# VectorE's gated convolution rows and FFN rows ahead of and between the two scans of their step (Mamba layer, one core)

## The chip, the core and the metric

The kernel is one launch on one core of a Trainium2 chip. A core has TensorE (PE in the rows; PEld is its loading of weights), VectorE (DVE), ScalarE (ACT), GpSimd (POOL) and SyncE (SP, which issues transfers here). Each engine works through a list of its own in order; they meet only through semaphores. The metric is the device time of one execution in microseconds (us).

## What is computed

Two layers run over x of 8 sequences x 512 positions x 128 channels, all float32. The first (attention with a gated score, and a mixture of experts) is not touched. The second is a Mamba block times the silu of a quantized FFN:

```python
xv = silu(causal_conv4(xn @ W_in) + conv_b)            # 256 inner channels
ssm = xv @ W_x                                          # 8 dt columns, 16 B, 16 C
delta = softplus(ssm[..., :8] @ W_dt + b_dt)
dA = exp(delta[..., None] * A)                          # A = -exp(A_log), 16 states
dBx = delta[..., None] * B[:, :, None, :] * xv[..., None]
h[t] = dA[t] * h[t-1] + dBx[t]                          # the scan, along the sequence
s = (einsum('bldn,bln->bld', h, C) + xv * D) @ W_out
g = silu((silu(xn @ wg) * (xn @ wu)) @ wd)
x = x + s * g
```

## The kernel before

The Mamba layer handles one sequence b a **round**: round -1 only prepares, rounds 0 to 7 scan, round 8 only ends the last. `rounds` (L1096) writes rounds -1 and 0 out, then a hardware loop whose body is two rounds (executed twice: rounds 1 to 4), then rounds 5, 6, 7 and 8. A round that scans b also **prepares** b+1 (`prep`, rounds 0 to 6: projection by W_x, softplus, delta, du) and **ends** b-1 (`end`, from round 1 on: the last two states and the output).

A round has NP = 8 **steps** q, with two states each (n = 2q and 2q+1) and two halves h of the inner channels. In step q:

- GpSimd multiplies B (replicated over the partitions) with du into `dbx`, two instructions (L1226, out `nfT_all`), one for each half. Between them it has to do, for the round before, three sums of `accP` (L1155) and the output in three instructions (L1163, L1167, L1171), and for the next round `softplus_high` at q = 5 (L1180, waits for ScalarE's `lg`), `softplus_low` at q = 6 (L1184, waits for ScalarE's `e1`, printed `e`), `deltas` at q = 7 (L1192) and `drives`, which makes du, last (L1200).
- ScalarE makes the decays `dA` in PSUM (`decays`, L1394), a step ahead: those of step q+1, two for each half. There are two buffers, so the decays of a half wait for the scan of that half in step q. Behind them in its list stand `scale_state` (L1431, states 5, 7, 9 and 15), `ffn_tanh` (L1444) and parts of the softplus (L1478, L1484, L1488).
- VectorE scans: two instructions (L1644, `TENSOR_TENSOR_SCAN`, out `xnT_all`, a ring of R = 4), one for each half. **Scan 0** and **scan 1** of a step below are these two.
- TensorE projects the states of step q by W_out (`project`, out psum, in `xnT_all`) once both halves are scanned, in step q+1 of its list, 16 matmuls a state (32 in the records, which show each float32 matmul of this size as two). VectorE adds each projected state, times its C column, to `acc` (`add_state`, L1660, four instructions). `project(n)` reuses the bank of state n-2 and waits until that is drained.

Two more kinds of VectorE work are what the change moves:

- **The gated convolution rows**: `conv_gate(h)` (L1670) makes `xv` of sequence b+1 from the tanh and the biased value that ScalarE left (`conv_silu`, L1418 and L1421, semaphore `yh`), one instruction for each half. `conv_silu(., 1)` waits for TensorE's `x_in(., 1)` (psum from `W_taps`), the last thing but the projections of states 14 and 15 in TensorE's round. From `xv` TensorE makes first `ssm()` (W_x), then `skip()` (W_outD), and only then, in step 1, projects states 0 and 1.
- **The FFN rows**: `ffn_hidden(k)`, k = 0, 1, 2 in steps q = 3, 4, 5 (L1710 and L1714), makes block k of the hidden layer from TensorE's `ffn_up(k)` (psum from `wgu`) and ScalarE's tanh `tf` of it. `ffn_up(k+1)` waits for `hf` k+1, that is for L1714; so does `ffn_down` (psum from `wd`) for all three.

The order in each engine's list is written out by hand in the loops over q; the loop of VectorE is the last part of its `round_`.

Of the kernel before, what the change touches and what calls it, by code (L numbers as in the profile page):

```python
# [5 lines left out]
def attention_moe_mamba_ffn(nc, t, out):  # L6
# [25 lines left out]
    KH = DI // P  # L32
# [10 lines left out]
    with ctx:  # L43
# [985 lines left out]
        with ExitStack() as ph:  # L1029
# [547 lines left out]
            def _(dve):  # L1577
# [51 lines left out]
                def round_(b, p, scan, prep, ahead, end):  # L1629
                    def w(n, c):  # L1630
                        dve.wait_ge(S[n], at(b + 1, n, c))

                    def ws(n, c):
                        dve.wait_ge(S[n], at(b, n, c))

                    def scans(q):
                        if not scan:
                            return
                        for h in range(KH):
                            i = 2 * q + h  # L1640
                            ws("dA", i + 1)
                            ws("dbx", i + 1)
                            ws("G", 2 * (q + 1 - 2))
                            nc.vector.tensor_tensor_scan(hring[:, i % R, :, :].rearrange("p n l -> p (n l)"),  # L1644
                                                         dA[:, i % RA, :, :].rearrange("p n l -> p (n l)"),
                                                         dbx[:, i % R, :, :].rearrange("p n l -> p (n l)"),
                                                         0.0, ALU.mult, ALU.add).then_inc(S["scan"], 1)

                    def add_state(b, p, m):

                        dve.wait_ge(S["G"], at(b, "G", m + 1))
                        if m == 0:
                            dve.wait_ge(S["acc0"], at(b, "acc0", 1))
                            dve.wait_ge(S["C"], at(b, "C", 1))
                            dve.wait_ge(S["os"], at(b - 2, "os", 1))
                        i = ON_DVE.index(m)
                        for j in range(TPB):
                            if i:
                                dve.wait_ge(S["acc"], at(b, "acc", (i - 1) * TPB + j + 1))
                            nc.vector.scalar_tensor_tensor(acc[:, p, j, :], bank[Gb[m % 2]][:, j * P:(j + 1) * P],  # L1660
                                                           Cc[:, p, j, m:m + 1],
                                                           acc[:, p, j, :] if i else skip_sb[:, p, j, :],
                                                           ALU.mult, ALU.add).then_inc(S["acc"], 1)

                    def conv_gate(h):
                        if h == 0:
                            w("acc_ps", 0)
                            w("du", 0)
                        w("yh", h + 1)
                        nc.vector.scalar_tensor_tensor(xv[:, h, :], tc_[:, h, :], 1.0, bank[bM[h]],  # L1670
                                                       ALU.add, ALU.mult).then_inc(S["xv"], 1)
# [35 lines left out]
                    def ffn_hidden(k):  # L1707
                        ws("tf", k + 1)
                        ws("hf", k)
                        nc.vector.scalar_tensor_tensor(fa[:, :], tf[:, :], 1.0, bank[bM[0]], ALU.add, ALU.mult)\  # L1710
                            .then_inc(S["fa"], 1)
                        ws("fa", k + 1)
                        ws("dn_ps", 0)
                        nc.vector.scalar_tensor_tensor(hff[:, k, :], fa[:, :], 0.5, bank[bM[1]], ALU.mult, ALU.mult)\  # L1714
                            .then_inc(S["hf"], 1)

                    def gate():
                        ws("tg", 1)
                        dve.wait_ge(S["og"], at(b - 1, "og", 0))
                        nc.vector.scalar_tensor_tensor(G1[:, p, :], tg[:, :], 1.0, bank[bM[1]], ALU.add, ALU.mult)\  # L1720
                            .then_inc(S["G1"], 1)
# [23 lines left out]
                    for q in range(NP):  # L1745
                        if q == 0 and not end:
                            conv_gate(0)
                            conv_gate(1)
                        scans(q)
                        if scan and 3 <= q < 6:  # L1750
                            ffn_hidden(q - 3)
                        if q == 0:
                            if prep and end:
                                conv_gate(0)
                                conv_gate(1)
                            if end:
                                for m in (NS - 2, NS - 1):
                                    if m in ON_DVE:
                                        add_state(b - 1, 1 - p, m)
                        elif scan:  # L1760
                            for m in (2 * q - 2, 2 * q - 1):
                                if m in ON_DVE:
                                    add_state(b, p, m)
                        if scan and q == 6:
                            gate()
# [7 lines left out]
                moments(1)  # L1773
                residual(3)
                rounds(dve, round_)

        run.close()  # L1777
# [41 lines left out]
```

## Time and profile before

| | us |
|---|---|
| median of 3 runs | 787.35 (785.91 to 788.26) |
| the profiled execution, its own time | 789.01 |
| its span, first to last instruction | 787.2 |
| TensorE busy | 667.2 |
| VectorE busy | 664.6 |
| GpSimd busy | 504.5 |
| ScalarE busy | 480.7 |
| layer 2, from round 1 on: VectorE's start of round 1, and the end of the span | 387.08, 787.2 |

The profile is of one execution. Busy time counts only the engine's own operations. A timeline row merges like instructions that follow each other: start, length in us, engine, line, operation, out<-in, count, and in brackets how long the engine sat idle just ahead of it and what released it. Two instructions merged into one row take less than twice the length of one, because the next starts a little before the end of the last: a pair of scans lasts 4.46 and the second starts 2.19 behind the first.

### The profile page before, as it was taken

What the parts mean: (1) busy time and instruction counts of PE and PEld (TensorE: products, weight loads), DVE (VectorE), ACT (ScalarE), POOL (GpSimd) and SP (SyncE); (2) the same over time, 40 slices, a digit from 0 to 9 for tenths busy, and PEclk for the clock granted to TensorE, in tenths of its full rate; (3) what the DMA queues carried; (4) which work ended last, traced back from release to release, by engine and by line L of the source; (5) the groups of instructions that cost most, each with busy time, mean ns of one, the idle gap of its engine ahead of it and who ended that gap; (6) DMA issues with size and microseconds to landing.
All of it is one profiled execution on the core that took longest, in us unless ns stands there. A gap on an engine that the chain in (4) does not pass through costs nothing. (4 is left out here: it accounts for less than half of the span.)

```text
span 787.2 us, 13531 instructions
## 1 busy us (share of the span) xinstructions
PE 667.2 (85%) x3984; PEld 495.5 (63%) x3984; DVE 664.6 (84%) x1182; ACT 480.7 (61%) x942; POOL 504.5 (64%) x292
## 2 busy tenths in 40 slices
PE   1889889999899928797998988888989979987882
PEld 0865556566565513466777777677767768777682
DVE  5968867777566638899999999899999999999992
ACT  1655656666344434978587585685695785874540
POOL 1002661000244552099999999989999999999952
PEclk9999999999999966989999999999999999998896
DMA  8800110003022244622032042042041230420000
GB/s 217 258 1 15 41 40 13 0 0 83 26 74 67 63 69 57 214 109 81 28 130 74 30 148 81 4 148 79 11 164 53 83 116 31 128 76 28 14 1 14
DMA packets 40199, 56.48 MB, mean 72 GB/s; under 512 B 5960, under 2 KB 30032, under 8 KB 40144
## 3 DMA queue, kind: packets, MB, share of 16 engines
q1 hardware_dynamic: 31888, 48.42, 19.1%
q0 software_dynamic: 6528, 6.84, 3.9%
q10 hardware_dynamic: 1728, 0.57, 0.4%
q8 instruction: 24, 0.39, 0.2%
q14 instruction: 31, 0.25, 0.1%
HBM read 46.08 MB, written 9.74 MB: 71 GB/s over the span
## 5 line engine op out<-in xcount | busy, mean ns | idle before, releaser
L1644 DVE TENSOR_TENSOR_SCAN xnT_all<-psum,nfT_all 128x1024 f32<-128x1024 f32 x128 | 285.3, 2270 | 2.7 <-issue 2.4
L1241 PEld LDWEIGHTS psum<-W_out,xnT_all 128*128 128x128 f32 x2048 | 243.8, 196 | 31.0 <-issue 29.0
L1241 PE MATMUL psum<-W_out,xnT_all 128*128 128x128 f32 x2048 | 246.0, 280 | 9.0 <-DVE acc L1660 9.0
L1394 ACT ACTIVATE psum<-delta,A 128x511 f32<-128x511 f32 x256 | 163.3, 678 | 39.2 <-DVE xnT_all L1644 38.4
L1226 POOL TENSOR_TENSOR nfT_all<-nf_rows,du 128x1024 f32<-128x1024 f32 x63 | 146.8, 2358 | 32.7 <-DVE nfT_all L1703 31.5
L1226 POOL TENSOR_TENSOR nfT_all<-attn_all,du 128x1024 f32<-128x1024 f32 x64 | 149.9, 2366 | 0.0
L569 POOL DMA_INDIRECT moe_dram<-xnT_all x40 | 38.3, 957 | 122.2 <-ACT xnT_all L825 122.2
L1660 DVE SCALAR_TENSOR_TENSOR acc<-psum,Cc,acc 128x128 f32<-128x128 f32 x352 | 96.7, 340 | 8.8 <-PE psum L1241 8.8
L558 POOL DMA_INDIRECT xs_dram<-nf_rows,pos x32 | 33.5, 1046 | 75.8 <-DVE pos L879 57.0
L1241 PE MATMUL psum<-vo_all,wgu 128*128 128x512 f32 (+1 forms) x96 | 47.6, 619 | 27.4 <-DVE hff L1714 27.4
L1241 PE MATMUL psum<-vo_all,W_taps 128*128 (+4 forms) x128 | 60.3, 619 | 1.4 <-ACT vo_all L1412 0.7
L618 PEld LDWEIGHTS psum<-vo_all,PT 128*128 128x128 f32 x256 | 31.9, 195 | 25.0 <-ACT PT L777 18.0
L1431 ACT ACTIVATE ts<-psum,Cc 128x128 f32<-128x128 f32 x128 | 35.7, 357 | 13.2 <-PE psum L1241 13.2
L695 PE MATMUL psum<-gud,xnT_all 128*128 x80 | 43.1, 623 | 0.5 <-ACT xnT_all L812 0.5
L1241 PEld LDWEIGHTS psum<-vo_all,wgu 128*128 128x128 f32 x96 | 16.5, 191 | 41.8 <-issue 26.0
L1241 PEld LDWEIGHTS psum<-vo_all,W_taps 128*128 128x128 f32 x128 | 24.3, 199 | 27.8 <-issue 25.8
L618 PE MATMUL psum<-vo_all,PT 128*128 (+1 forms) x256 | 37.7, 291 | 2.6 <-ACT PT L777 2.6
L1418 ACT ACTIVATE tconv<-psum,convb 128x512 f32<-128x512 f32 x16 | 11.0, 687 | 42.7 <-PE psum L1241 42.7
L994 DVE COPY xnT_all<-psum 128x256 f32<-128x256 f32 x40 | 17.0, 424 | 23.4 <-PE psum L707 23.4
L588 PE MATMUL psum<-k_w,q_w 128*128 128x512 f32 x64 | 33.5, 608 | 0.0
L1155 POOL TENSOR_TENSOR accP<-accP,ts 128x512 f32<-128x512 f32 x16 | 20.3, 1271 | 18.0 <-ACT ts L1431 18.0
L1241 PE MATMUL psum<-wd,hff 128*128 128x128 f32 x192 | 23.6, 279 | 8.8 <-DVE hff L1714 8.8
(209 smaller groups left out, 1139.2 us busy)
## 6 DMA issues: line engine op xcount, KB each, us to landing
nf_rows<-bt_dram SPq DMA_DIRECT2D x32, 512.0 KB, 5.2
attn_all<-bt_dram SPq DMA_DIRECT2D x32, 512.0 KB, 3.5
xs_dram<-attn_all SPq DMA_DIRECT2D x4, 645.0 KB, 8.6
xnT_all<-xs_dram SPq DMA_DIRECT2D x40, 64.5 KB
x_all<-in_x_dram SPq DMA_DIRECT2D x8, 256.0 KB, 7.0
res_all<-moe_dram POOLq DMA_DIRECT2D x8, 256.0 KB, 4.5
out_dram<-ow SPq DMA_DIRECT2D x8, 256.0 KB, 2.4
gud<-in_gate_dram SPq DMA_DIRECT2D x1, 1024.0 KB, 5.9
```

The source lines that it names most:

```text
L558: pool.indirect_dma_start(xs_dram, bass.IndirectOffsetOnAxis(ap=pos[:, i:i + 1], axis=0), nf_rows[:, i, :], None).then_inc(s_sc, 16)
L569: pool.indirect_dma_start(moe_dram, bass.IndirectOffsetOnAxis(ap=xs_t[:, u % XN, D:ROW].bitcast(u32), axis=0), yt[:, u % UN, :], None).the ...
L588: nc.tensor.matmul(bank[j % 2], q_w[:, j * P:(j + 1) * P], k_w[:, :], start=True, stop=True)\
L618: ins = nc.tensor.matmul(bank[4][:, j * P:(j + 1) * P], PT[:, j % 2, c, :], vo_all[:, ds(b * TPB + c, 1), :], start=(c == 0), stop=(c == T ...
L695: nc.tensor.matmul(bank[2 + u % 2], xT[:, u % 2, :], gud_flat[:, ds(expert[u], 2 * I)], start=True, stop=True).then_inc(E["gu_ps"], 1)
L1155: nc.gpsimd.tensor_tensor(accP[:, :, :], ts[:, 0, :, :] if i == 1 else accP[:, :, :], ts[:, i, :, :], ALU.add).then_inc(S["accP"], 2 if i ...
L1226: nc.gpsimd.tensor_tensor(dbx[:, i % R, :, :], B_pair(q), du[:, p, h:h + 1, :].to_broadcast([P, 2, L]), ALU.mult)\
L1241: return nc.tensor.matmul(o, l, r, start=start, stop=stop)
L1394: ins = nc.scalar.activation(dA[:, i % RA, k, 1:L], delta[:, p, h, 1:L], ACT.Exp, scale=A[:, h, 2 * q + k:2 * q + k + 1])
L1431: ins = nc.scalar.activation(ts[:, i, j, :], bank[Gb[n % 2]][:, j * P:(j + 1) * P], ACT.Copy, scale=Cc[:, p, j, n:n + 1])
L1644: nc.vector.tensor_tensor_scan(hring[:, i % R, :, :].rearrange("p n l -> p (n l)"), dA[:, i % RA, :, :].rearrange("p n l -> p (n l)"), dbx ...
L1660: nc.vector.scalar_tensor_tensor(acc[:, p, j, :], bank[Gb[m % 2]][:, j * P:(j + 1) * P], Cc[:, p, j, m:m + 1], acc[:, p, j, :] if i else s ...
```

## The change

VectorE's scans of a step are written one half at a time. In step 0 of the rounds that both end a sequence and prepare one (1 to 6), `conv_gate(0)` goes ahead of scan 0 and `conv_gate(1)` between the scans; in steps 3 to 5 of every scanning round `ffn_hidden` goes between the scans. Round 0, which has both `conv_gate` calls ahead of its scans, keeps them there. No instruction is added or taken away, and no other engine's list changes.

```diff
-                    def scans(q):
+                    def scans(q, halves):
                         if not scan:
                             return
-                        for h in range(KH):
+                        for h in halves:
                             i = 2 * q + h
...
                         if q == 0 and not end:
                             conv_gate(0)
                             conv_gate(1)
-                        scans(q)
+                        if q == 0 and prep and end:
+                            conv_gate(0)
+                        scans(q, (0,))
+                        if q == 0 and prep and end:
+                            conv_gate(1)
                         if scan and 3 <= q < 6:
                             ffn_hidden(q - 3)
+                        scans(q, (1,))
                         if q == 0:
-                            if prep and end:
-                                conv_gate(0)
-                                conv_gate(1)
                             if end:
                                 for m in (NS - 2, NS - 1):
```

VectorE's list of the kernel before at the start of round 5, the first behind the loop. `p6_yh` is ScalarE's signal for a convolution half, `p6_dA` and `p6_dbx` are the two inputs of a scan, `p6_G` is TensorE's projection.

```order
L1644 SCALAR_TENSOR_TENSOR xnT_all<-psum,nfT_all 128x1024 [waits p6_G,p6_dbx,p6_dA] x2
L1670 SCALAR_TENSOR_TENSOR xv<-tconv,psum 128x512 [waits p6_yh,p6_du,p6_acc_ps]
L1670 SCALAR_TENSOR_TENSOR xv<-tconv,psum 128x512 [waits p6_yh]
L1660 SCALAR_TENSOR_TENSOR acc<-psum,Cc,acc 128x128 [waits p6_acc,p6_G]
L1660 SCALAR_TENSOR_TENSOR acc<-psum,Cc,acc 128x128 [waits p6_acc] x3
```

The same place in the changed kernel:

```order
L1670 SCALAR_TENSOR_TENSOR xv<-tconv,psum 128x512 [waits p6_yh,p6_du,p6_acc_ps]
L1644 SCALAR_TENSOR_TENSOR xnT_all<-psum,nfT_all 128x1024 [waits p6_G,p6_dbx,p6_dA]
L1670 SCALAR_TENSOR_TENSOR xv<-tconv,psum 128x512 [waits p6_yh]
L1644 SCALAR_TENSOR_TENSOR xnT_all<-psum,nfT_all 128x1024 [waits p6_G,p6_dbx,p6_dA]
L1660 SCALAR_TENSOR_TENSOR acc<-psum,Cc,acc 128x128 [waits p6_acc,p6_G]
L1660 SCALAR_TENSOR_TENSOR acc<-psum,Cc,acc 128x128 [waits p6_acc] x3
```

Each convolution row stands one scan earlier than before or more (the first two scans, the second one), and the wait on `p6_yh` of the second half now stands ahead of scan 1.

Steps 3 and 4 of a round in the kernel before (the scans' signals as above; `p6_tf` is ScalarE's tanh for the FFN):

```order
L1644 SCALAR_TENSOR_TENSOR xnT_all<-psum,nfT_all 128x1024 [waits p6_G,p6_dbx,p6_dA] x2
L1710 SCALAR_TENSOR_TENSOR fa<-tf,psum 128x512 [waits p6_hf,p6_tf]
L1714 SCALAR_TENSOR_TENSOR hff<-fa,psum 128x512 [waits p6_dn_ps,p6_fa]
L1660 SCALAR_TENSOR_TENSOR acc<-psum,Cc,acc 128x128 [waits p6_acc,p6_G]
L1660 SCALAR_TENSOR_TENSOR acc<-psum,Cc,acc 128x128 [waits p6_acc] x3
```

And step 3 in the changed kernel:

```order
L1644 SCALAR_TENSOR_TENSOR xnT_all<-psum,nfT_all 128x1024 [waits p6_G,p6_dbx,p6_dA]
L1710 SCALAR_TENSOR_TENSOR fa<-tf,psum 128x512 [waits p6_hf,p6_tf]
L1714 SCALAR_TENSOR_TENSOR hff<-fa,psum 128x512 [waits p6_dn_ps,p6_fa]
L1644 SCALAR_TENSOR_TENSOR xnT_all<-psum,nfT_all 128x1024 [waits p6_G,p6_dbx,p6_dA]
L1660 SCALAR_TENSOR_TENSOR acc<-psum,Cc,acc 128x128 [waits p6_acc,p6_G]
L1660 SCALAR_TENSOR_TENSOR acc<-psum,Cc,acc 128x128 [waits p6_acc] x3
```

The pair of FFN rows stands one scan earlier, and scan 1 one pair later.

## Rows read from the trace of the kernel before

**Rows 1.** The page, its busy times and shares of the span.
```profile
PE 667.2 (85%) x3984; PEld 495.5 (63%) x3984; DVE 664.6 (84%) x1182; ACT 480.7 (61%) x942; POOL 504.5 (64%) x292
```
**Rows 2.** Busy time by stretch: round 4: us, then PE, PEld, DVE, ACT, POOL.
```profile
553.88:608.64 54.76, 50.04 (x338) 40.25 (x337) 53.23 (x75) 39.61 (x69) 54.01 (x27) 1.00 0.24 82
```
**Rows 3.** VectorE's timeline in round 4, and the start of round 5.
```profile
553.88 4.46 DVE L1644 TENSOR_TENSOR_SCAN xnT_all<-psum,nfT_all 128x1024 f32<-128x1024 f32 x2
558.26 1.26 DVE L1670 SCALAR_TENSOR_TENSOR xv<-tconv,psum 128x512 f32<-128x512 f32 x2
...
565.33 1.13 DVE L1660 SCALAR_TENSOR_TENSOR acc<-psum,Cc,skip_sb 128x128 f32<-128x128 f32 x4 [0.40 <-PE psum L1241]
567.21 1.13 DVE L1660 SCALAR_TENSOR_TENSOR acc<-psum,Cc,acc 128x128 f32<-128x128 f32 x4 [0.76 <-PE psum L1241]
...
574.69 4.46 DVE L1644 TENSOR_TENSOR_SCAN xnT_all<-psum,nfT_all 128x1024 f32<-128x1024 f32 x2
579.07 0.66 DVE L1710 SCALAR_TENSOR_TENSOR fa<-tf,psum 128x512 f32<-128x512 f32 x1
579.76 0.69 DVE L1714 SCALAR_TENSOR_TENSOR hff<-fa,psum 128x512 f32<-128x512 f32 x1
...
600.57 1.12 DVE L1660 SCALAR_TENSOR_TENSOR acc<-psum,Cc,acc 128x128 f32<-128x128 f32 x4 [0.27 <-PE psum L1241]
...
608.64 4.46 DVE L1644 TENSOR_TENSOR_SCAN xnT_all<-psum,nfT_all 128x1024 f32<-128x1024 f32 x2
```
**Rows 4.** TensorE's timeline in round 4.
```profile
559.61 1.91 PE L1241 MATMUL psum<-xv,W_x 128*40 128x512 f32 x4
...
563.34 3.74 PE L1241 MATMUL psum<-W_out,xnT_all 128*128 128x128 f32 x32
...
587.21 1.98 PE L1241 MATMUL psum<-vo_all,wgu 128*128 x4 [1.16 <-DVE hff L1714]
...
593.92 2.94 PE L1241 MATMUL psum<-wd,hff 128*128 128x128 f32 x24 [1.16 <-DVE hff L1714]
```
**Rows 5.** ScalarE's timeline in round 4.
```profile
556.87 0.66 ACT L1421 ACTIVATE psum<-psum,convb 128x512 f32<-128x512 f32 x1
...
582.52 0.60 ACT L1444 ACTIVATE tf<-psum 128x512 f32<-128x512 f32 x1
...
584.10 1.06 ACT L1488 ACTIVATE e<-e 128x1024 f32<-128x1024 f32 x1
...
592.61 1.30 ACT L1394 ACTIVATE psum<-delta,A 128x511 f32<-128x511 f32 x2 [0.88 <-DVE xnT_all L1644]
593.85 1.12 ACT L1431 ACTIVATE ts<-psum,Cc 128x128 f32<-128x128 f32 x4
```
**Rows 6.** GpSimd's timeline, rounds 3 and 4.
```profile
523.06 2.35 POOL L1180 TENSOR_TENSOR lg<-lg,rl 128x1024 f32<-128x1024 f32 x1 [2.02 <-ACT lg L1478]
...
568.75 4.68 POOL L1226 TENSOR_TENSOR nfT_all<-nf_rows,du 128x1024 f32<-128x1024 f32 x2
...
585.23 2.36 POOL L1184 TENSOR_TENSOR e<-ab,e 128x1024 f32<-128x1024 f32 x1 [0.19 <-ACT e L1488]
```
**Rows 7.** Who waited for whom, all of layer 2 (us, times, longest).
```profile
POOL lg L1180 <- ACT lg L1478: 3.0, 2, 2.0
POOL e L1184 <- ACT e L1488: 1.8, 5, 0.5
```
**Rows 8.** Who waited for whom on VectorE, from 370 us on.
```profile
DVE acc L1660 <- PE psum L1241: 10.8, 21, 2.1
```
**Rows 9.** VectorE at the loop's second pass, the start of round 3.
```profile
499.16 4.47 DVE L1644 TENSOR_TENSOR_SCAN xnT_all<-psum,nfT_all 128x1024 f32<-128x1024 f32 x2 [2.40 <-issue]
```
**Rows 10.** GpSimd's timeline in round 0.
```profile
356.36 2.35 POOL L1180 TENSOR_TENSOR lg<-lg,rl 128x1024 f32<-128x1024 f32 x1 [0.99 <-ACT lg L1478]
...
363.82 2.36 POOL L1184 TENSOR_TENSOR e<-ab,e 128x1024 f32<-128x1024 f32 x1 [0.46 <-ACT e L1488]
```
**Rows 11.** The timeline of round 7, step 3: GpSimd's products and VectorE's scans.
```profile
732.62 4.68 POOL L1226 TENSOR_TENSOR nfT_all<-nf_rows,du 128x1024 f32<-128x1024 f32 x2
...
736.55 4.46 DVE L1644 TENSOR_TENSOR_SCAN xnT_all<-psum,nfT_all 128x1024 f32<-128x1024 f32 x2
```

## The prediction

> **What bounds the kernel now.** I read first the busy shares [rows 1]. Over the span they say little: two layers are mixed in them, and the change touches the second alone. So next the busy time by round [rows 2]: in round 4, 54.76 us long, VectorE is busy 53.23 and GpSimd 54.01, TensorE 50.04 and ScalarE 39.61. Two engines are full at once, and the question is which of them leads and how far the other lies behind.
>
> VectorE's timeline [rows 3] shows three idle pieces in the round, all waits for TensorE's projections: 0.40 ahead of state 0, 0.76 ahead of state 1, 0.27 ahead of state 11, 1.43 in all. Over the layer such waits come to 10.8 us in 21 pieces [rows 8]; 2.1 of it, the longest, is the last state of the kernel, which the change doesn't reach. VectorE never waits for GpSimd.
>
> GpSimd's timeline [rows 6] shows the other side. It waits not for VectorE's scans but for ScalarE's softplus parts: 4.8 us in seven pieces [rows 7]. 1.45 of that is in round 0 [rows 10]. The rest, 3.35, is 2.02 for `lg` in round 3 [rows 6], and four waits of 0.2 to 0.4 for `e1` in rounds 3 to 6 (1.8 less 0.46). The 2.02 has a source: at the loop's second pass VectorE stands still 2.40 with nothing that it waits for [rows 9], ScalarE's decays wait for its scans, and `lg` comes late. So GpSimd is drawn along by VectorE through ScalarE, with little play. The play the other way is larger: in round 4, step 3, the product for scan 0 ends at 568.75 + 2.34 = 571.09 and the scan starts at 574.69, 3.6 us later [rows 3, 6]. In round 7, step 3, it is 732.62 + 2.34 = 734.96 against 736.55, 1.6 us [rows 11]. VectorE leads today; GpSimd takes over once VectorE has gained these.
>
> **FFN rows between the scans (steps 3 to 5, rounds 0 to 7).** Each pair costs what it cost, 1.29 us from start to start (579.07 to about 580.36) [rows 3], and ends one scan, 2.19, earlier. Scan 1 ends 1.29 later; the add behind it starts when it did. The first gain is TensorE's, which idles until L1714 ahead of `ffn_up(1)`, `ffn_up(2)` (1.16) and `ffn_down` (1.16) [rows 4]. With the rows 2.19 earlier, `ffn_down` waits instead for its own predecessor: `project(8)` has to wait for scan 1 of step 4 and the add that drains state 6, about 588.2, against 589.0 before. I work out 1.9 us earlier for `ffn_down`, and 1.75 for what follows, since `project(10)` then waits for the add of state 8. From there to state 1 of the next round TensorE has no idle time of note, so all of that chain moves: state 11's wait (0.27) goes, `x_in(., 1)` and `yh` come 1.4 earlier relative to VectorE, and the waits for states 0 and 1 (0.40, 0.76) go if the convolution rows are in time too.
>
> What hides scan 1's delay: its decays and TensorE's projections. Queued behind the decays that wait for scan 1 stand `scale_state` and then the tanh for the next FFN pair. Its chain is: scan 1 ends, +0.04, decays to 1.24 later, the scaling 1.12, the tanh 0.60 [rows 5], with gaps 3.1 us. The next FFN row is reached after the add (1.04) and scan 0 (2.19), 3.15 us behind scan 1's end. It fits by 0.05. I take no wait, and keep 0.3 a pair as the other bound.
>
> The same chain carries `e1`. In rounds 0 (nothing gained yet) its last operation, at 584.10 in the pattern round, comes 0.3 to 0.4 later, since the decays now start at scan 1's end: GpSimd's wait of 0.46 in round 0 becomes 0.8 [rows 5, 10]. **Cost: +0.33 on GpSimd, once.** Later rounds have VectorE ahead by more.
>
> **Convolution rows around scan 0 (rounds 1 to 6).** They cost 1.18 as before. `xv` is complete at 553.88 + 0.59 + 2.19 + 0.67 = 3.45 us into the round instead of 5.65. TensorE was free for `ssm()` only at 559.61, 5.73 in [rows 4], so by themselves these rows gain nothing; with TensorE 1.4 ahead it arrives at 4.3 and finds them ready, and state 0 is projected at 9.98 (needed 10.98), state 1 at 11.86 (needed 12.0). The new wait is on `yh` of half 1, ready at 556.87 + 0.66 = 557.53 [rows 5] and now asked for at 556.66: 0.9 too late without TensorE's lead, 0.5 early with it. Behind it on VectorE stands scan 1, and the decays and scaled state 15 behind that. I take nothing, with 0.9 a round as the bound.
>
> **VectorE's sum**: 1.43 a round gained in six rounds and 0.2 to 0.3 in rounds 0 and 7, nearly 9 us. That would hold only with GpSimd out of the way.
>
> **GpSimd's sum.** Its work is the same. With VectorE and ScalarE ahead of it, its waits of rounds 3 to 6 go: 3.35; round 0 costs 0.33. At round 7 it is 3.0 earlier. The 2.40 of the loop's second pass [rows 9] stays on VectorE, but by then VectorE has gained some 3, `lg` is early enough, and the stall no longer reaches GpSimd. VectorE runs into GpSimd at step 3 of round 4 or 5 (3.6 of play plus 2.0 of GpSimd's own gain against 1.43 a round), and is held by it from there. The narrowest place is round 7, step 3: 1.6 of play and 3.0 gained is 4.6 earlier. Behind it GpSimd has no more softplus to make and draws away, and state 11's 0.2 comes on top. **Total: 4.8 us.** The profiled execution took 789.01, 1.7 above the median of 787.35; the sum is made on its rows, 789.01 - 4.8 = 784.2, and carried to the median 787.35 - 4.8 = 782.6.
>
> The Trainium skill (Runtime: NRT & Kernel Launch, Instruction fetch mechanics) says that a taken branch to code outside the fetched window stalls the engine until that code is there. By that rule the trace agrees as to VectorE (2.40 at the loop's second pass), but it would allow GpSimd a stall of its own at its branch.
>
> **Rivals.**
>
> *A stall of GpSimd's own.* GpSimd ran over its branch with VectorE's stall in front of it. If a like stall of 2.4 showed on GpSimd once it leads, the time would be 785.0. Against it: the trace has no such idle piece on GpSimd in either pass. The page named above is the rule behind it. Chance 0.06.
>
> *The waits only change place.* If `ffn_down` doesn't come earlier (TensorE held by the drains, or the tanh late), the convolution row of half 1 waits 0.9 ahead of scan 1, the states' waits of 1.16 shrink by as much, and what is left is 0.1 to 0.5 a round: 784.5 to 787. For it: 0.05 and 0.14 us of play in two places. Against it: TensorE's 1.16 and 1.16 idle before L1714's users. Chance 0.16, two thirds of it within 0.3%.
>
> *Slower: the FFN rows wait for the tanh between the scans.* If the chain behind scan 1 is longer than 3.15 by w, VectorE waits w twice a round, eight rounds, and each wait delays scan 1 and so the next chain. It eats the gain at w = 0.7 and makes the kernel slower by 0.3% (2.4 us) at w of about 0.85; at 1.0 it ends near 790 to 791. For it: the chain and the distance are equal to within 0.05. Against it: every piece of the chain is a row with a stable length. Chance 0.06.
>
> *GpSimd is not the limit*, and VectorE's whole gain comes through, 779. Its products would have to be there 4 us before the rows say. Chance 0.02.
>
> **How the numbers follow.** The forecast, GpSimd-bound at 782.6, has the remaining 0.70; its own range is 781.4 to 784.0 (play read at two places to 0.3, up to 0.5 lost to late tanhs in round 7, and the median's own scatter of about 1). The rivals at 785.0 and part of those to 787 are taken in up to 785.6. A measurement of this kernel can tell about 0.3%, 2.4 us: faster means below 785.0. Forecast 0.70, half of the first rival, a third of the second and the last give 0.80 for faster; 0.13 the same; 0.07 slower.
>
> **What the changed profile would show.** VectorE's waits for TensorE fall from 10.8 us to about 3 (the last state and the first round's rest); waits for GpSimd's products appear in their place, some 3 to 5 us, first in step 3 of round 4 or 5 and at last in step 3 of round 7, and nothing behind it. GpSimd's waits for `lg` and `e1` after round 0 are gone, and the one in round 0 for `e1` is about 0.8. TensorE idles less than 0.5 ahead of `ffn_down`. The 2.40 at the loop's second pass is still there. I am wrong if a wait for `yh` stands ahead of scan 1 in rounds 2 to 6, if L1710 waits for `tf` by more than 0.3, or if GpSimd still waits for ScalarE in rounds 4 to 6.

## The result, and the profile after

The changed kernel takes 782.32 us (median of 20 runs, 777.96 to 785.51), the kernel before 787.35 (median of 20). The ratio is 0.9939, 95% interval 0.9926 to 0.9951: 0.6% faster. The forecast was 782.6, with 781.4 to 784.0 as its own range and up to 785.6 with the rivals.

The profiled execution of the changed kernel took 780.33 (span 778.5), that of the kernel before 789.01 (787.2). That is 8.7 us apart, more than the medians, because the first layer, which the change doesn't touch, was 3.4 us shorter in the second of these executions. So I read **layer 2** alone: from the first `conv_gate` row of round 0 to the end of the span. It starts at 334.13 before and at 330.77 after, and lasts 453.1 and 447.7 us: 5.3 less.

The waits that end on VectorE, all behind 370 us, in the changed kernel (us in total, times, longest); they answer to [rows 8]:

```profile
DVE xnT_all L1644 <- issue: 4.2, 4, 1.5
DVE acc L1660 <- PE psum L1241: 2.6, 1, 2.6
DVE xv L1670 <- ACT psum L1421: 2.3, 1, 2.3
DVE xnT_all L1644 <- POOL nfT_all L1226: 0.2, 1, 0.2
```

The waits for TensorE have gone from 10.8 us in 21 pieces to one piece of 2.6, the last state of the kernel. The 2.3 is the standstill of the loop's second pass [rows 9]: it now falls on the first operation of round 3, a convolution row, and is put down to ScalarE, whose half 1 came at that moment (492.48, the row starts at 492.51); but that row waits for half 0, which had been there since 485.56, for 7 us. What is new are the 4.2 ahead of L1644, without a releaser. VectorE's timeline shows where they are:

```profile
565.73 2.29 DVE L1644 TENSOR_TENSOR_SCAN xnT_all<-psum,nfT_all 128x1024 f32<-128x1024 f32 x1 [0.57 <-issue]
...
619.98 2.29 DVE L1644 TENSOR_TENSOR_SCAN xnT_all<-psum,nfT_all 128x1024 f32<-128x1024 f32 x1 [1.11 <-issue]
...
674.21 2.29 DVE L1644 TENSOR_TENSOR_SCAN xnT_all<-psum,nfT_all 128x1024 f32<-128x1024 f32 x1 [1.06 <-issue]
...
713.82 4.60 DVE L1644 TENSOR_TENSOR_SCAN xnT_all<-psum,nfT_all 128x1024 f32<-128x1024 f32 x2 [0.23 <-POOL nfT_all L1226]
...
728.39 2.29 DVE L1644 TENSOR_TENSOR_SCAN xnT_all<-psum,nfT_all 128x1024 f32<-128x1024 f32 x1 [1.48 <-issue]
```

The four put down to issue are scan 0 of step 3 in rounds 4, 5, 6 and 7; the one put down to GpSimd, 0.23, is scan 0 of step 1 in round 7. Beside three of the four, GpSimd's products of the same steps:

```profile
563.28 4.68 POOL L1226 TENSOR_TENSOR nfT_all<-nf_rows,du 128x1024 f32<-128x1024 f32 x2
...
617.54 4.68 POOL L1226 TENSOR_TENSOR nfT_all<-nf_rows,du 128x1024 f32<-128x1024 f32 x2
...
725.93 4.68 POOL L1226 TENSOR_TENSOR nfT_all<-nf_rows,du 128x1024 f32<-128x1024 f32 x2
```

The first product of a pair ends 2.34 after the start: 565.62, 619.88, 728.27. Each scan starts 0.1 later. I read these as waits for GpSimd, whatever the row names; an experiment below tests it.

GpSimd's own waits for ScalarE, from round 0 on, against [rows 7]:

```profile
POOL lg L1180 <- ACT lg L1478: 1.2, 1, 1.2
POOL e L1184 <- ACT e L1488: 0.6, 1, 0.6
```

Seven pieces have become two, both in round 0. And TensorE around `ffn_down` in round 4, against [rows 4]:

```profile
569.38 1.98 PE L1241 MATMUL psum<-vo_all,wgu 128*128 x4 [0.89 <-DVE hff L1714]
572.60 3.84 PE L1241 MATMUL psum<-W_out,xnT_all 128*128 128x128 f32 x32 [1.24 <-DVE acc L1660]
576.27 1.88 PE L1241 MATMUL psum<-vo_all,wgu 128*128 x4
579.31 3.84 PE L1241 MATMUL psum<-W_out,xnT_all 128*128 128x128 f32 x32 [1.16 <-DVE acc L1660]
582.98 2.84 PE L1241 MATMUL psum<-wd,hff 128*128 128x128 f32 x24
```

`ffn_down` (the last) no longer waits for L1714; what TensorE mostly waits for is the add that drains a bank.

### The profile page after: what moved, and what is told of

The parts are those of the page before. It is cut to its first block and busy times, and to the rows that moved or that the text cites. A ratio compares the mean times of both kernels' runs of the same rounds, so it can differ in the third digit from the quotient of the medians.

```text
span 778.5 us, 13531 instructions
## 1 busy us (share of the span) xinstructions
PE 666.0 (86%) x3984; PEld 492.5 (63%) x3984; DVE 663.7 (85%) x1182; ACT 480.7 (62%) x942; POOL 503.4 (65%) x292
## 5 line engine op out<-in xcount | busy, mean ns | idle before, releaser
L1644 DVE TENSOR_TENSOR_SCAN xnT_all<-psum,nfT_all 128x1024 f32<-128x1024 f32 x128 | 288.5, 2275 | 4.7 <-issue 4.2
L1394 ACT ACTIVATE psum<-delta,A 128x511 f32<-128x511 f32 x256 | 165.5, 680 | 93.5 <-DVE xnT_all L1644 93.4
L1241 PE MATMUL psum<-vo_all,wgu 128*128 128x512 f32 (+1 forms) x96 | 45.9, 600 | 6.8 <-DVE hff L1714 6.8
L695 PE MATMUL psum<-gud,xnT_all 128*128 x80 | 43.7, 631 | 0.4 <-ACT xnT_all L812 0.4
L812 ACT ACTIVATE xnT_all<-psum 128x128 f32<-128x128 f32 x40 | 11.0, 277 | 32.2 <-PE psum L681 32.2
L609 PE MATMUL psum<-const,PR 128*128 128x128 f32 x128 | 20.3, 282 | 10.7 <-ACT PR L771 10.7
L719 PE MATMUL psum<-gud,xnT_all 128*128 x160 | 28.0, 297 | 1.5 <-DVE xnT_all L994 1.5
```

The source lines that it names most:

```text
L695: nc.tensor.matmul(bank[2 + u % 2], xT[:, u % 2, :], gud_flat[:, ds(expert[u], 2 * I)], start=True, stop=True).then_inc(E["gu_ps"], 1)
L719: ins = nc.tensor.matmul(bank[6 + u % 2][:, 0:D], hT[:, u % 2, k, :], gud_flat[:, ds(expert[u] + (2 * I + k * D), D)], start=(k == 0), sto ...
L1241: return nc.tensor.matmul(o, l, r, start=start, stop=stop)
L1394: ins = nc.scalar.activation(dA[:, i % RA, k, 1:L], delta[:, p, h, 1:L], ACT.Exp, scale=A[:, h, 2 * q + k:2 * q + k + 1])
```

## The experiments

Twelve runs of eleven kernels (one was run twice), all of them against the kernel before. Because effects of 1 to 3 us are near what a ratio can tell, each row has layer 2 of its profiled execution too, read as above. The last column is the part of that difference that has come about by the start of the last pair of scans (step 7 of round 7: 763.99 before, 755.56 in the changed kernel).

| kernel | ratio (95%) | layer 2, us | less than before | up to the last scans |
|---|---|---|---|---|
| changed | 0.9939 (0.9926 to 0.9951) | 447.7 | 5.3 | 5.1 |
| FFN rows only | 0.9980 (0.9957 to 1.0003) | 450.5 | 2.6 | 2.6 |
| convolution rows only | 0.9959 (0.9942 to 0.9977) | 451.8 | 1.3 | 1.2 |
| the same again | 0.9973 (0.9956 to 0.9991) | 450.8 | 2.3 | 0.7 |
| changed, both convolution rows first | 0.9971 (0.9953 to 0.9989) | 451.4 | 1.7 | 1.6 |
| changed, less GpSimd work | 0.9836 (0.9810 to 0.9862) | 442.7 | 10.3 | 10.3 |
| before, less GpSimd work | 0.9994 (0.9978 to 1.0010) | 453.5 | -0.4 | -0.4 |
| before, loop written out | 0.9971 (0.9954 to 0.9989) | 450.0 | 3.1 | 3.1 |
| changed, loop written out | 0.9921 (0.9901 to 0.9941) | 446.5 | 6.6 | 6.5 |
| changed, a sum on VectorE | 1.0028 (1.0000 to 1.0056) | 459.9 | -6.8 | -5.8 |
| changed, that sum with one input in PSUM | 0.9920 (0.9891 to 0.9950) | 446.3 | 6.8 | 6.8 |
| changed, GpSimd's output spread | 0.9871 (0.9844 to 0.9898) | 443.0 | 10.1 | 10.0 |
| both: spread, loop written out | 0.9841 (0.9817 to 0.9865) | 440.8 | 12.3 | 10.7 |

What stands behind the last pair of scans, to the end of the span, took 22.9 to 23.2 us in eleven of the fourteen traces, the one before among them, but 21.6 in two ("the same again" and the last row) and 24.3 in "a sum on VectorE". The change doesn't reach it; TensorE's last state is projected there. The same 32 matmuls in "convolution rows only":

```profile
765.20 5.38 PE L1241 MATMUL psum<-W_out,xnT_all 128*128 128x128 f32 x32 [3.49 <-DVE acc L1660]
```

and in "the same again":

```profile
767.73 3.81 PE L1241 MATMUL psum<-W_out,xnT_all 128*128 128x128 f32 x32 [3.49 <-DVE acc L1660]
```

The granted clock of this last stretch was 0.83 and 0.84 in the two short traces, 0.66 in the long one and 0.71 to 0.77 in the others. So I compare two traces by the last column. One kernel traced twice differs there by 0.5 us (1.2 and 0.7); the ratios of neighbouring rows mostly overlap.

**Which half of the change carries it?** The first kernel puts `conv_gate(0)` and `(1)` back behind the scans:

```diff
-                        if q == 0 and prep and end:
-                            conv_gate(0)
                         scans(q, (0,))
-                        if q == 0 and prep and end:
-                            conv_gate(1)
...
                         if q == 0:
+                            if prep and end:
+                                conv_gate(0)
+                                conv_gate(1)
```

> Only the FFN rows stand between the scans (steps 3 to 5); the convolution rows stay behind both scans of step 0, as before. Theory (TensorE's lead must meet an early xv): TensorE leaves the FFN part 1.7 us earlier but then waits for xv, ready 5.7 us into the round as before, so the waits ahead of states 0 and 1 stay (0.4 and 0.8) and only state 11's 0.27 goes: 0.3 us in each of 8 rounds, 1.5 to 2.5 us less than before, ratio 0.997 to 0.998; TensorE waits about 1.4 us for L1670. Rival (the FFN rows carry the gain alone): 4 to 5 us, ratio 0.994.

0.9980, and 2.6 us in layer 2, as expected; by the ratio alone, which reaches 1.0003, no gain is not excluded. TensorE's waits show the lead being thrown away:

```profile
PE psum L1241 <- DVE xv L1670: 9.3, 6, 3.5
```

It reaches `ssm()` early in all six rounds and stands there for `xv`. On VectorE the waits ahead of states 0 and 1 are as before; only state 11's is gone:

```profile
562.73 1.13 DVE L1660 SCALAR_TENSOR_TENSOR acc<-psum,Cc,skip_sb 128x128 f32<-128x128 f32 x4 [0.36 <-PE psum L1241]
564.61 1.13 DVE L1660 SCALAR_TENSOR_TENSOR acc<-psum,Cc,acc 128x128 f32<-128x128 f32 x4 [0.76 <-PE psum L1241]
```

The second kernel is the other half, `ffn_hidden` back behind both scans:

```diff
-                        if scan and 3 <= q < 6:
-                            ffn_hidden(q - 3)
                         scans(q, (1,))
+                        if scan and 3 <= q < 6:
+                            ffn_hidden(q - 3)
```

> Only the convolution rows are moved ahead of and between the scans of step 0; the FFN rows stay behind both scans. Theory: TensorE reaches ssm no earlier than 5.7 us into the round, and the row of half 1 is asked for 0.9 us before ScalarE has its value: VectorE waits 0.8 to 0.9 there, the waits ahead of states 0 and 1 shrink from 1.16 to 0.3 in exchange, and the time stays, ratio 0.999 to 1.001. Rival (the convolution rows carry the gain): 4 to 5 us, ratio 0.994.

The mechanism is there as expected, VectorE in round 4 and at its end:

```profile
553.46 0.69 DVE L1670 SCALAR_TENSOR_TENSOR xv<-tconv,psum 128x512 f32<-128x512 f32 x1 [0.81 <-ACT psum L1421]
563.11 1.12 DVE L1660 SCALAR_TENSOR_TENSOR acc<-psum,Cc,acc 128x128 f32<-128x128 f32 x4 [0.35 <-PE psum L1241]
596.46 1.12 DVE L1660 SCALAR_TENSOR_TENSOR acc<-psum,Cc,acc 128x128 f32<-128x128 f32 x4 [0.27 <-PE psum L1241]
608.21 0.69 DVE L1670 SCALAR_TENSOR_TENSOR xv<-tconv,psum 128x512 f32<-128x512 f32 x1 [0.81 <-ACT psum L1421]
```

0.81 + 0.35 + 0.27 is the 1.43 of before: the wait has moved from TensorE's states to ScalarE's value, and the round still lasts 608.21 - 553.46 = 54.75. But the kernel was not the same: 0.9959. One microsecond I had overlooked: in round 3 the loop's standstill comes ahead of the convolution rows, the value of half 1 is ready by its end, and the waits of 1.1 ahead of states 0 and 1 of that round are gone too. For the rest I measured the kernel once more.

> The kernel with only the convolution rows moved, once more, on another chip job: its trace accounts for 1.3 us in layer 2 (ratio 0.998), its ratio was 0.9959 (0.9942 to 0.9977). Theory (the rest is scatter of the first layer): 0.997 to 0.9995. Rival (the rows alone give 3 us): 0.995 to 0.997.

0.9973 (0.9956 to 0.9991), layer 2 shorter by 2.3. The ratio is in the theory's range, but its interval reaches into the rival's. Of the 2.3 only 0.7 is there by the last pair of scans, against 1.2 in the first trace; the other 1.6 is the faster last stretch shown above. So this half alone is worth about 1 us, which is what round 3 gives, and my expectation of nothing was wrong by that. The two ratios say 2 to 3 us; what they hold beyond that 1 us has no counterpart in the rows.

**Where must the row of half 1 stand?** Both rows ahead of scan 0:

```diff
                         if q == 0 and prep and end:
                             conv_gate(0)
+                            conv_gate(1)
                         scans(q, (0,))
-                        if q == 0 and prep and end:
-                            conv_gate(1)
```

> The changed kernel with both convolution rows ahead of scan 0 in rounds 1 to 6 (as round 0 has them). Theory: the row of half 1 is now asked for 0.6 us into the round, ScalarE has its value at 2.3: a wait of 1.6 to 1.8 a round, VectorE gains nothing a round (1.43 less 1.7), and the time is that of the kernel before within 1.5 us, ratio 0.998 to 1.002. Rival (VectorE's slack against GpSimd hides it): ratio 0.994 as changed.

0.9971 (0.9953 to 0.9989), and 1.7 us in layer 2, between the two. The wait is as forecast, 1.72 or 1.78 in every round but the third:

```profile
DVE xv L1670 <- ACT psum L1421: 11.0, 6, 2.3
```

It eats the gain but not quite all; again the third round's wait hides in the standstill. The place between the scans is worth 3.6 us against it.

**Is GpSimd the limit after, and was it not before?** The same cut in both kernels:

```diff
-                        nc.gpsimd.tensor_tensor(lg[:, :, :], lg[:, :, :], rl[:, :, :], ALU.add).then_inc(S["sp"], 1)
+                        nc.gpsimd.tensor_tensor(lg[:, :, 0:64], lg[:, :, 0:64], rl[:, :, 0:64], ALU.add).then_inc(S["sp"], 1)
```

> The changed kernel, with GpSimd's softplus_high (L1180, 2.35 us) on 128 of its 1024 columns: it leaves out the rest of that sum, some 2 us of GpSimd's work in each of rounds 0 to 6. Theory (GpSimd limits the changed kernel from round 4 on; the five idle pieces ahead of L1644, 4.4 us in all, that the trace puts down to issue or GpSimd are waits for its products): these pieces go and the time falls by about 4 more, ratio 0.989 to 0.990. Rival (those pieces are VectorE's own, fetching code): they stay, ratio 0.994.

> The kernel before with the same part of GpSimd's softplus_high left out. Theory: GpSimd doesn't limit the kernel before, VectorE's three waits for TensorE a round stay as they are: ratio 0.999 to 1.001. Rival (GpSimd already limits it): 2 us in each of 7 rounds would come back in part, 4 us or more, ratio under 0.995.

On the kernel before it does nothing (0.9994): GpSimd takes its shorter sum and waits for ScalarE instead (`e1` 15.5 us in all where it was 1.8). On the changed kernel the five pieces ahead of L1644 vanish. VectorE's whole list of waits behind 370 us is then:

```profile
DVE xv L1670 <- issue: 2.2, 1, 2.2
DVE acc L1660 <- PE psum L1241: 1.9, 1, 1.9
```

Layer 2 is 5.0 shorter than the changed kernel's, for 4.4 of waits. So the pieces named issue were GpSimd's. The ratio, 0.9836 (0.9810 to 0.9862) from six executions, fell further than the expected 0.989. The medians, 787.88 and 777.24, are 10.6 apart, which the 10.3 of layer 2 accounts for; what the ratio says beyond that, 2 us, has no counterpart in the trace and stays open.

**The loop's standstill.** The hardware loop becomes a Python loop that writes rounds 1 to 4 out:

```diff
-                with eng.Fori(0, (NB - 4) // 2) as r:
+                for r in range((NB - 4) // 2):
```

> The kernel before with the hardware loop over rounds 1 to 4 written out; nothing else. Theory (the 2.40 us that VectorE stands still at the loop's second pass is on the path of the kernel before, and draws GpSimd along): the piece goes and the time falls by 2.0 to 2.5 us, ratio 0.997. Rival (it is covered): no change, 0.9995 to 1.0005.

> The changed kernel with the loop written out. Theory (VectorE's stall is covered by GpSimd's work in the changed kernel): only GpSimd's own gaps in the loop's rounds count, 0.2 to 0.5 us each that rounds 5 and 6 don't show: 0.3 to 1.3 us less than the changed kernel, ratio to the kernel before 0.992 to 0.994, and VectorE's waits for GpSimd's products grow by 1 to 2 us. Rival (the stall costs the changed kernel as much): 2.4 us, ratio 0.991.

On the kernel before 0.9971, as expected, where the 2.40 is on the path; its layer 2 is 3.1 shorter, 0.7 more than the standstill, and VectorE's waits for TensorE (10.8 to 10.4) and its one wait for a decay (0.3) make up that rest. On the changed kernel it gives 1.2 us in layer 2 (1.4 by the last scans), so about half of the 2.3 was covered. The ratio, 0.9921 (0.9901 to 0.9941), holds the theory and the rival's 0.991 alike; it is the trace that decides. There the waits for GpSimd grow from 4.4 to 5.4 us, the standstill's share taking another name.

**Taking work off GpSimd.** If GpSimd limits rounds 4 to 7, one of its sums could go to VectorE in rounds 5 and 6:

```diff
-                                sum_scaled(b, 1)
+                                if not (isinstance(b, int) and b in (5, 6)):
+                                    sum_scaled(b, 1)
...
+                        if q == 5 and isinstance(b, int) and b in (5, 6):
+                            sum_first()   # accP = ts[0] + ts[1] on VectorE
```

> The changed kernel, with the first sum of accP (L1155, 1.23 us on GpSimd) made by VectorE in rounds 5 and 6, in step 5 behind its add; the result is the same. Theory (GpSimd limits rounds 4 to 7): GpSimd is 2.46 us earlier at round 7, VectorE pays 0.65 twice out of its 4.4 us of waits: 2 to 2.5 us less than the changed kernel, ratio to the kernel before 0.990 to 0.991. Rival (VectorE still limits, or an operation with both inputs in SBUF is held up by GpSimd's running product for up to 2.3 us): no gain or 1 to 3 us lost, ratio 0.994 to 0.998.

No gain but a loss: 1.0028 (1.0000 to 1.0056), 0.9% above the changed kernel, more than the rival said. The trace is of the longest of its twelve executions (795.09, median 790.20), so the table's 6.8 us overstates the usual loss. VectorE's two rows of this sum, in that execution:

```profile
642.60 10.38 DVE L1669 TENSOR_TENSOR accP<-ts 128x512 f32<-128x512 f32 x1
...
707.10 2.81 DVE L1669 TENSOR_TENSOR accP<-ts 128x512 f32<-128x512 f32 x1
```

and GpSimd beside the first:

```profile
638.51 4.70 POOL L1227 TENSOR_TENSOR nfT_all<-attn_all,du 128x1024 f32<-128x1024 f32 x2
643.16 2.35 POOL L1192 TENSOR_TENSOR delta<-e,lg 128x1024 f32<-128x1024 f32 x1
645.48 4.65 POOL L1227 TENSOR_TENSOR nfT_all<-attn_all,du 128x1024 f32<-128x1024 f32 x2
650.09 2.34 POOL L1200 TENSOR_TENSOR du<-delta,xv 128x1024 f32<-128x1024 f32 x1
655.34 4.66 POOL L1227 TENSOR_TENSOR nfT_all<-nf_rows,du 128x1024 f32<-128x1024 f32 x2 [2.92 <-DVE xnT_all L1645]
```

VectorE's sum starts at 642.60 and ends at 652.98, half a microsecond after GpSimd's last operation in a row, at 652.43. GpSimd had four operations back to back from 643.16 on, and the sum ended only when GpSimd stood still itself, because it needed a scan that VectorE had not been able to start. I had allowed for one operation of 2.3. The Trainium skill (SBUF — State Buffer, SBUF: two separate sides) says that VectorE and GpSimd share a pair of ports that the one holds for a whole instruction while the other blocks, and that a VectorE operation with two inputs in SBUF needs it beside a GpSimd operation that reads SBUF. The rows agree as to the kind, and show more than one instruction's wait: 10.38 us beside operations of 2.3. So the last test of this kind: the same size of sum, one input in PSUM (the edit shortened; GpSimd's own sum stays out in both rounds).

```diff
+                        if k == 2 and isinstance(b, int) and b in (5, 6):
+                            ws("ts", 2)
+                            dve.wait_ge(S["og"], at(b - 1, "og", 1))
+                            nc.vector.tensor_tensor(accP, ts[0], bank[bM[0]], ALU.add).then_inc(S["accP"], 2)
```

> As the kernel with the accP sum on VectorE in rounds 5 and 6, but the sum adds a row of PSUM to the first scaled state instead of the second scaled state (it leaves that state out), so that only one input lies in SBUF, and it stands inside the last FFN pair. Theory (the sum with both inputs in SBUF was held up by GpSimd's running products, 10.38 and 2.81 us for 0.69 us of work): it now takes 0.7 us in both rounds and the time is 1 to 2.5 us under the changed kernel's, ratio 0.991 to 0.993. Rival (the sum waits for something else, such as the output of the round before): it still takes several us in one of the rounds, ratio 1.000 or more.

```profile
634.42 0.69 DVE L1718 TENSOR_TENSOR accP<-ts,psum 128x512 f32<-128x512 f32 x1
```

0.69 in both rounds, beside a running product of GpSimd (634.10 to 638.78), and 0.9920 (0.9891 to 0.9950). The sum keeps its waits for `ts` and for the output, so those were not what made it long, and the input in PSUM fits the account by the ports. But the row also stands at another place of the step; input and place were changed together, and no run tells them apart. Two sums fewer on GpSimd are worth 1.4 us in layer 2 (1.7 by the last scans), a difference that the two ratios can't tell.

**Spreading GpSimd's work.** The rows said that GpSimd is late at one place of a round, step 3, where the output's three instructions stand. The edit, shortened:

```diff
                             if q == 1 and end:
-                                sum_scaled(b - 1, 2)
+                                sum_scaled(b - 1, 1)
+                            if q == 2 and end:
+                                sum_scaled(b - 1, 2)
                             if q == 3 and end:
                                 sum_scaled(b - 1, 3)
-                                output()
+                                output(0)     # L1163
+                            if q == 4 and end:
+                                output(1)     # L1167
+                            if q == 5 and end:
+                                output(2)     # L1171
...
-                                sum_scaled(b, 1)      # in step 7
```

> The changed kernel with GpSimd's sums and output spread out: the first sum of accP goes from step 7 to step 1 of the next round, the second to step 2, the third and L1163 stay in step 3, L1167 goes to step 4 and L1171 to step 5; the same work, the same result. Theory (GpSimd's total doesn't change, but it is late at the narrow places, step 3 of rounds 4 to 7 and the start of round 7): its products of step 7 and of the next step 0 come 1.2 us earlier, those of step 3 2.5, and 2.5 to 3 us of VectorE's waits go: ratio to the kernel before 0.990 to 0.991. Rival (its total alone counts, the waits turn up in other steps): 0.994 as the changed kernel.

> The same spreading, and the loop over rounds 1 to 4 written out. Theory: the two gains add, 2.5 to 3 us from the spreading and 1.2 from the gaps of the loop's rounds and the stall that is no longer covered by waits: ratio to the kernel before 0.987 to 0.990, the best of all. Rival (one limit behind both): no better than the better of the two alone, 0.990 to 0.992.

0.9871 (0.9844 to 0.9898) and 0.9841 (0.9817 to 0.9865): better than expected, and the lowest of the kernels that compute the full result (medians 775.13 and 773.80 us, against 786.93 for the kernel before on the same chip). With the spreading alone no wait of VectorE for GpSimd shows any more. Its waits behind 370 us:

```profile
DVE xv L1681 <- issue: 2.2, 1, 2.2
DVE acc L1671 <- PE psum L1252: 2.0, 1, 2.0
DVE xnT_all L1655 <- ACT psum L1405: 0.3, 1, 0.3
```

I had expected 2.5 to 3 of the 4.4 back; all of it came, and layer 2 is 4.7 shorter than the changed kernel's. With the loop written out too, layer 2 is 12.3 us shorter than before and VectorE waits 2.4 us in all behind 370. But 1.6 of these 12.3 is the faster last stretch; by the last pair of scans writing the loop out adds 0.7 to the spreading, not the expected 1.2, and the two ratios overlap, so that the gains add is not shown. VectorE meets GpSimd again there: its scan at 712.82 stands idle for 0.22, and the product ends at 710.37 + 2.34 = 712.71. The spreading was not tried on the kernel before. That it would give nothing there is argued from the shorter sum, which gave nothing.

## Why the prediction was right

**FFN rows.** Shown. Behind 370 us TensorE's waits for L1714 shrank from 32.6 us to 6.6; its waits for draining adds grew from 9.0 to 30.2 in their place, as worked out, so its idle time fell little, but its work came earlier. `ffn_down` starts 582.98 - 545.56 = 37.42 us into round 4 where it started at 593.92 - 553.88 = 40.04. Without the 1.16 of states 0 and 1 and the 0.57 that VectorE waited for GpSimd, that is 2.0 earlier; 1.9 was forecast. Alone these rows are worth 2.6 us.

**Convolution rows.** The sum gave them nothing by themselves and let them depend on TensorE's lead. The halves show that: 2.6 and about 1 us apart, 5.3 together, and 10.3 once GpSimd is out of the way (the changed kernel with less GpSimd work; VectorE's sum had said nearly 9). "By themselves these rows gain nothing" was off by that 1 us, in round 3. The new wait on `yh` is absent with the lead (the value is there at 547.92, asked for at 548.36: 0.44 early, 0.5 forecast) and 0.81 without it (0.9 forecast).

**The tanh behind scan 1.** No L1710 waits in the changed kernel, in any round. The play was larger than the 0.05 of the forecast. In round 4:

```profile
573.79 0.61 ACT L1444 ACTIVATE tf<-psum 128x512 f32<-128x512 f32 x1
...
574.65 0.66 DVE L1710 SCALAR_TENSOR_TENSOR fa<-tf,psum 128x512 f32<-128x512 f32 x1
```

The tanh ends at 574.40, 0.25 ahead of the row. Scan 1 ended at 571.52, so the distance is 3.13 (3.15 forecast), but the chain is 2.88 and not 3.1: the tanh starts 1.00 behind the start of the scaling, which the sum had at 1.12 with gaps on top. That the forecast of no wait held does not rest on 0.05.

**GpSimd's sum.** From round 0's first product to that of step 3 in round 7 GpSimd took 732.62 - 334.45 = 398.17 before and 725.93 - 331.09 = 394.84 after: 3.3 less, 3.0 forecast. The cost in round 0 was 0.17 for `e1` (0.46 to 0.63), half of the 0.33 forecast, and 0.23 for `lg` (0.99 to 1.22), which the forecast had left out; together 0.40, near it by luck. VectorE reached that scan in 728.39 - 330.77 = 397.62 where it took 736.55 - 334.13 = 402.42: 4.8 less, 4.6 forecast. Its idle pieces come first in round 4, step 3, and last in round 7, step 3. It had touched GpSimd once before, in round 2, step 3, where the product ends at 454.06 + 2.34 = 456.40 and the scan starts at 456.52; the loop's standstill then set it back. The rest of the 5.3 lies behind that (0.5; 0.2 forecast), half of it in the last stretch, whose length changes from execution to execution.

**The rivals.** GpSimd showed no stall of its own at its branch. "The waits only change place" failed too: `ffn_down` did come earlier, and no wait for `yh` stands ahead of scan 1 in any round. The slower one would have needed a chain longer by 0.25, not by 0.05.

What I misjudged lies outside the sum: I took GpSimd's total as the limit behind its narrow place, and it was the order of its work. "VectorE's whole gain comes through" was given 779 and 0.02; the same work on GpSimd in another order gives more than that.

## What to carry to other kernels

When two engines are each 97 to 99% busy, find which waits for which, and how many microseconds the leader can gain before it meets the other. Here the gain was the smallest distance between a product's end and its use (1.6 us, late in the kernel) plus what the other engine gained itself (3.3). Then look at what stands ahead of that narrowest step on the other engine; spreading those instructions cost nothing and gave as much again as the change itself. And two moves that are worth 2.6 and about 1 us alone can be worth 5 together, and 10 once the next limit is out of the way, if one makes the lead and the other uses it: don't drop either for what it gives alone. When a few microseconds are at stake, compare traces up to a point that the change can reach; here the last stretch alone varied by up to 2.7 us.

## What the hardware showed that I had not expected

- A VectorE operation with both inputs in SBUF, 0.69 us of work, took 10.38 us beside GpSimd operations that followed each other, and 2.81 in another round; the same size with one input in PSUM, at another place of the step, took 0.69 both times. The kernel with it scattered from 784.33 to 795.09, and the 10.38 is from the execution of 795.09.
- An idle piece without a releaser can be a wait for GpSimd: four of them, 0.57 to 1.48, ended 0.1 behind GpSimd's product, and went when GpSimd had less to do.
- Writing the loop out was worth 0.3% on the kernel before, for a standstill of 2.40 us in one of its two passes.
- The last stretch of the kernel, which no edit touches, took 21.6 to 24.3 us. The last 32 matmuls took 3.81 us in a trace with a granted clock of 0.83 in that stretch, and 5.38 in one of the same kernel with 0.77.
